# Attention inside a macaron block: the results of a pair of heads are normalised, turned and split in front of the second half of the next pair's keys

## The chip, the cores and the metric

The kernel runs on one core of a Trainium2 chip. The metric is the device time of one execution in microseconds; the lower the better. Engine names in the profile: PE is TensorE, PEld its weight load, DVE VectorE, ACT ScalarE, POOL GpSimd, SP SyncE, which here only issues DMAs.

## What is computed

x has 8 batch rows of 1024 tokens with 256 features. A feed-forward block (fp4-quantised weights and activations) is followed by attention and a second feed-forward block; each adds to x:

```python
x = x + 0.5 * ffn(layernorm(x))
x = x + attn(layernorm(x))
x = x + 0.5 * ffn(layernorm(x))
```

Attention has 16 heads of 64:

```python
q, k, v = heads(query @ Wq), heads(query @ Wk), heads(query @ Wv)
w = softmax(einsum('bhqd,bhkd->bhqk', q, k) / DH + causal)
w = w * mask                                  # a ramp over keys, one span for each head
w = w / (sum(w) + 1e-8)
out = einsum('bhqk,bhkd->bhqd', w, v)
return merge_heads(out) @ Wo
```

## The kernel before

The first feed-forward block (and the preparation of weights) takes the first 580 us, attention the stretch to about 2870 us, the second block the rest. All engines' programs are written out by hand; each engine runs its own list in order, and semaphores tie them together.

**Pairs.** Attention goes over 8 batch rows, and in each over 8 pairs of heads (`over_pairs`): 64 pairs, numbered g. A pair is a fixed list of steps that `pair_steps` makes and that TensorE, ScalarE and VectorE all read, each doing its own part of it. GpSimd and SP have lists of their own (`pair` in their blocks).

**Units and groups.** A pair has 16 units: a head a and a block j of 128 queries, in the order `ORDER`. A unit's keys (causal, so j + 1 blocks) are cut into groups of up to four blocks; `GROUPS` has 24 of them for a pair. For a unit, TensorE makes scores two units ahead (`scores`, L1398 and L1399), VectorE takes the row maximum (`row_max`, L1591), ScalarE the exponential (`exp`, L1499). For a group, TensorE transposes the exponentials (`turn`, L1409), ScalarE and VectorE split them into fp16 high and low halves (`turn_hi` L1507, `turn_lo` L1597), and TensorE multiplies with the values three groups later (`value`, L1425, LAG = 3). ScalarE copies finished results to `o_raw` (`copy_out`, L1518). The last results of a pair are thus copied behind the third group of the next.

**Side pieces.** Between these run the pieces that prepare the next pair g + 1 and finish the pair g - 1. All use one PSUM bank, `side_ps`, one after the other. A piece sits in a slot: the number of the group behind whose transposes TensorE takes it (`V_SLOTS`, `WO_SLOTS`, `FRESH_SLOTS`, filled in order by the list `pieces`). The pieces are:
- q, k: projections of the next pair's queries and keys, two halves of 512 tokens each (L1323). ScalarE copies a half to SBUF as it is (`keep_raw`, L1474), GpSimd splits it into high and low halves (`split`, L1277 and L1279), and SP places both by DMA where the scores read them (`place`, L1141): 4 DMAs for q, 8 for k, when both halves are split.
- o_turn: transposes of the normalised results of g - 1, two halves (L1364), with the same way over ScalarE and GpSimd into `oT`. The first half waits for the semaphore o_norm.
- v: the value projection for the next two pairs (L1335), in every second pair ("V pairs", odd g). wo: the output product with Wo (L1376), in the others ("W pairs", even g); its first piece waits for both halves of oT.
- x_turn: transposes of the next batch row's x, in the pair r = 6 of all batch rows but the last (`turns_rows`). These 7 are W pairs too and use `FRESH_SLOTS`, with 14 pieces.

**The result path.** When ScalarE has copied the last results of g - 1, GpSimd adds their two parts (`sums`, L1255, o_sum). VectorE makes the denominators (`normalise`: den L1604, rden L1608) behind the groups named in `NORM`. GpSimd multiplies (`outputs`, L1260, o_norm), TensorE turns the result (o_turn), ScalarE copies, GpSimd splits. GpSimd does all this in the order of its own list, in which `outputs` waits for rden and each `split` for its raw copy:

```python
for kind, c in (("q", 0), ("q", 1), ("k", 0)):
    split(kind, c, g + 1, None, None)
outputs(g - 1)
split("k", 1, g + 1, None, None)
for c in range(2):
    split("o_turn", c, None, g - 1, 1 - par)
```

Of the kernel before, what the change touches and what calls it, by code (L numbers as in the profile page):

```python
# [581 lines left out]
ORDER = (7, 0, 5, 1, 6, 3, 4, 2)  # L582
UNITS = [(a, j) for a in range(2) for j in ORDER]
GROUPS = [(n, k0, min(GROUP, j + 1 - k0)) for n, (a, j) in enumerate(UNITS) for k0 in range(0, j + 1, GROUP)]
NORM = (6, 7)
ROWS_FROM = 11

WO_SLOTS = (0, 2, 4, 7, 9, 11, 14, 15, 19, 21)
# [18 lines left out]
def starts_rows(b, r):  # L607

    return isinstance(r, int) and r == 0 and not (isinstance(b, int) and b == BATCH - 1)


def turns_rows(b, r):

    return r == PAIRS - 2 and b < BATCH - 1


def pair_steps(before, after, fresh, values, rows=False):

    q, k, v, turn_o, wo, turn_x = ([(kind, c, dg) for c in range(n)] for kind, n, dg in (
        ("q", 2, 1), ("k", 2, 1), ("v", 4, 1), ("o_turn", 2, -1), ("wo", 4, -1), ("x_turn", 4, 1)))
    pieces = (q + k if after else [None] * 4) + (turn_x if fresh else []) + (turn_o if before else [None] * 2)
    if values:
        pieces += v if after else [None] * 4
    else:
        pieces += wo if before else [None] * 4  # L630
    slots = {i: [] for i in range(NG)}
    for i, piece in zip(FRESH_SLOTS if fresh else V_SLOTS if values else WO_SLOTS, pieces, strict=True):
        slots[i].append(piece)
    steps, late_lo = [], []

    def flush(late):
        steps.extend(late)
        late.clear()

    for n in range(NU):  # L640
        more = n + 2 < NU or after
        unit = ((n + 2) % NU, (n + 2) // NU)
        if more:
            steps.append(("scores",) + unit)
        for i in [i for i, (m, _, _) in enumerate(GROUPS) if m == n]:
            first = GROUPS[i][1] == 0
            if i >= LAG or before:
                steps.append(("value", (i - LAG) % NG, (i - LAG) // NG))
                m = GROUPS[(i - LAG) % NG][0]
                if LAST_GROUP[m] == (i - LAG) % NG:  # L650
                    steps.append(("copy", m, (i - LAG) // NG))
            steps.append(("turn", i, 0))
            if i or before:
                steps.append(("lo", (i - 1) % NG, (i - 1) // NG))
            flush(late_lo)
            if first and more:
                steps.append(("max",) + unit)
            for piece in slots[i]:
                flush(late_lo)
                if piece:  # L660
                    steps.append(piece)
                    steps.append((piece[0] + "_hi",) + piece[1:])
                    late_lo.append((piece[0] + "_lo",) + piece[1:])
            if first and more:
                steps.append(("exp",) + unit)
            if before and i in NORM:
                steps.append(("norm", NORM.index(i), -1))
            if rows and i >= ROWS_FROM:
                steps.append(("norm_x", i - ROWS_FROM, 1))
    flush(late_lo)  # L670
    if not after:
        steps.append(("lo", NG - 1, 0))
        for i in range(NG - LAG, NG):
            steps.append(("value", i, 0))
            if LAST_GROUP[GROUPS[i][0]] == i:
                steps.append(("copy", GROUPS[i][0], 0))
    return steps
# [392 lines left out]
def attention(nc, block, sem, sb, src, dst, dram, keep, given):  # L1070

    tail = {}
    with ExitStack() as ctx:
# [131 lines left out]
        def _(pool):  # L1205
# [16 lines left out]
            def root(n):  # L1222
                pool.wait_ge(sem("var_eps"), n)
                nc.gpsimd.tensor_tensor(rstd[:], var_eps[:], power[:], ALU.pow).then_inc(sem("rstd"), 1)

            def masks(g, r):

                if g is not None:

                    pool.wait_ge(sem("v_masked"), g * 2)  # L1230
                    pool.sem_inc(sem("passed_pool"), 1)
                nc.gpsimd.tensor_copy(twin_mask[:], keep["mask"][:, :, bass.ds(r * 2, 4)]).then_inc(sem("twin_mask"), 2)

            def values(g, r, par):

                vc = v_cols[par]

                pool.wait_ge(sem("value_done"), g * NG - NG + AHEAD["value_done"])
                pool.sem_inc(sem("passed_pool"), 1)
                nc.gpsimd.tensor_copy(vc[:, :, :, DH], keep["mask_hi"][:, :, bass.ds(r * 2, 2)]).then_inc(sem("v_edge"), 1)  # L1240
                nc.gpsimd.tensor_copy(vc[:, :, :, VHI + DH], keep["mask_lo"][:, :, bass.ds(r * 2, 2)]).then_inc(sem("v_edge"), 1)
                for c in range(2):

                    pool.wait_ge(sem("v_masked"), 2 * g + (2 * c + 2 - 2 * par))
                    pool.sem_inc(sem("passed_pool"), 1)
                    rows = slice(c * (QT // 2), (c + 1) * (QT // 2))
                    vm = v_masked[:, rows, 2 * par:2 * par + 2, :]
                    nc.gpsimd.tensor_copy(vc[:, rows, :, 0:DH], vm).then_inc(sem("v_hi"), 1)  # L1248
                    pool.wait_ge(sem("v_hi"), 2 * g + (c + 1))
                    nc.gpsimd.tensor_tensor(vc[:, rows, :, VHI:VHI + DH], vm, vc[:, rows, :, 0:DH], ALU.subtract).then_inc(sem("v_cols"), 1)  # L1250

            def sums(g):

                pool.wait_ge(sem("o_copied"), g * NO + (NO + AHEAD["o_copied"]))
                nc.gpsimd.tensor_tensor(o_sum[:], o_raw[:, :, :VHI], o_raw[:, :, VHI:], ALU.add).then_inc(sem("o_sum"), 1)  # L1255

            def outputs(g):

                pool.wait_ge(sem("rden"), g + 1)
                nc.gpsimd.tensor_tensor(o_norm[:].rearrange("p j a d -> p a j d"), o_sum[:, :, :DH].rearrange("p (a j) d -> p a j d", a=2),  # L1260
                                        rden[:].rearrange("p (a j) -> p a j", a=2).unsqueeze(3).broadcast_to([P, 2, QT, DH]),
                                        ALU.mult).then_inc(sem("o_norm"), 1)

            def split(kind, c, g, gp, par_p):

                if kind == "o_turn":
                    hi, lo = (oT[s][:, par_p, c * GROUP:(c + 1) * GROUP].rearrange("p j n -> p (j n)") for s in range(2))
                    names, count = ("oT_hi", "oT_lo"), 2 * gp + (c + 1)

                    pool.wait_ge(sem("wo_added"), 2 * gp - (2 if par_p else 0) + AHEAD["wo_added"])  # L1270
                    pool.wait_ge(sem("o_turn_raw"), 2 * gp + (c + 1))
                else:
                    hi, lo = (side[kind][s][:, c * CHUNK:(c + 1) * CHUNK] for s in range(2))
                    names, count = (f"{kind}_hi", f"{kind}_lo"), 2 * g + (c + 1)

                    pool.wait_ge(sem(f"{kind}_raw"), 2 * g - 2 + (c + 1))
                nc.gpsimd.tensor_copy(hi, side_raw[kind][:, c]).then_inc(sem(names[0]), 1)  # L1277
                pool.wait_ge(sem(names[0]), count)
                nc.gpsimd.tensor_tensor(lo, side_raw[kind][:, c], hi, ALU.subtract).then_inc(sem(names[1]), 1)  # L1279
# [6 lines left out]
            def pair(b, r, par, before, after, fresh, twin):  # L1286
                g = b * PAIRS + r
                if after and par == 1:
                    masks(g + 1, 0 if fresh else r + 1)
                if before:  # L1290
                    sums(g - 1)
                if after:
                    for kind, c in (("q", 0), ("q", 1), ("k", 0)):
                        split(kind, c, g + 1, None, None)
                if before:
                    outputs(g - 1)
                if after:
                    split("k", 1, g + 1, None, None)
                if before:
                    for c in range(2):  # L1300
                        split("o_turn", c, None, g - 1, 1 - par)
                if after:
                    values(g + 1, 0 if fresh else r + 1, 1 - par)
                if starts_rows(b, r):
                    root(b + 2)

            pool.sem_inc(sem("o_sum"), AHEAD["o_sum"])
            pool.sem_inc(sem("oT_lo"), AHEAD["oT_lo"])
            over_pairs(pool, start, pair)
            tail["gpsimd"] = {START: lambda: sums(BATCH * PAIRS - 1), -2: lambda: outputs(BATCH * PAIRS - 1)}  # L1310

# [429 lines left out]
```

## Time and profile before

| what | value |
|---|---|
| median of 3 runs | 3377.65 us (3376.19 to 3378.86) |
| the profiled execution | 3378.71 us, of it the profile's span 3376.6 us |
| busy over the span | PE 95%, PEld 79%, DVE 81%, ACT 70%, POOL 44% |
| mean granted TensorE clock | 0.987 of full speed |
| one W pair and one V pair together | 69.9 us |

How to read it: the share of an engine is an average over three stages; attention has to be read by itself. Waits are attributed to the instruction whose semaphore came last. Ends of matmuls are modelled, so starts are the safer numbers on TensorE. "issue" as the cause of a wait means that the profile shows no releaser. Slots and groups are not named in the rows; they follow from the order of the instructions.

### The profile page before, as it was taken

What the parts mean: (1) busy time and instruction counts of PE and PEld (TensorE: products, weight loads), DVE (VectorE), ACT (ScalarE), POOL (GpSimd) and SP (SyncE); (2) the same over time, 40 slices, a digit from 0 to 9 for tenths busy, and PEclk for the clock granted to TensorE, in tenths of its full rate; (3) what the DMA queues carried; (4) which work ended last, traced back from release to release, by engine and by line L of the source; (5) the groups of instructions that cost most, each with busy time, mean ns of one, the idle gap of its engine ahead of it and who ended that gap; (6) DMA issues with size and microseconds to landing.
All of it is one profiled execution on the core that took longest, in us unless ns stands there. A gap on an engine that the chain in (4) does not pass through costs nothing.

```text
span 3376.6 us, 77211 instructions
## 1 busy us (share of the span) xinstructions
PE 3196.7 (95%) x28848; PEld 2678.6 (79%) x28848; DVE 2747.1 (81%) x5326; ACT 2365.3 (70%) x4315; POOL 1500.9 (44%) x1666
## 2 busy tenths in 40 slices
PE   4999996999999999999999999999999998799998
PEld 4999995677777777777777777777777776799998
DVE  8999984877877887787787778878777777899996
ACT  3566652777777777778777777777777777465564
POOL 2243321544545545445445455455455453233331
PEclk9999998999999999999999999999999999899999
DMA  3133212222422332332233223224222333111110
GB/s 110 49 96 95 92 63 60 63 62 57 106 56 58 79 82 58 78 78 62 62 81 79 60 63 90 60 60 105 54 57 67 82 70 107 35 57 57 57 54 32
DMA packets 160353, 235.78 MB, mean 70 GB/s; under 512 B 30064, under 2 KB 71152, under 8 KB 159728
## 3 DMA queue, kind: packets, MB, share of 16 engines
q1 hardware_dynamic: 159984, 230.84, 26.0%
q8 instruction: 234, 3.83, 0.5%
q14 instruction: 135, 1.11, 0.1%
HBM read 95.49 MB, written 34.61 MB: 39 GB/s over the span
## 4 chain that ended last, share of the span: by engine, by line
PE 68%; issue 6%; DVE 5%; ACT 2%; POOL 2%; DVEq 0%; ACTq 0%; POOLq 0%
PE at_t_ps L1409 13%; PE at_o_ps L1425 10%; PE at_side_ps L1323 10%; PE ffn_gu_ps L505 7%; PE at_s_ps L1398 6%; PE at_s_ps L1399 6%; PE at_side_ps L1376 4%; PE ffn_down_ps L530 4%; PE at_side_ps L1335 4%; DVE at_e_rows L1591 2%; PE at_side_ps L1364 2%; ACT at_eT_hi L1507 1%; PE ffn_hT_ps L475 1%; DVE at_eT_lo L1597 1%; DVE at_v_masked L1569 1%
## 5 line engine op out<-in xcount | busy, mean ns | idle before, releaser
L1597 DVE SCALAR_TENSOR_TENSOR at_eT_lo<-at_t_ps,at_eT_hi 128x512 f16<-128x512 f32 (+3 forms) x1536 | 852.7, 555 | 471.5 <-ACT at_eT_hi L1507 445.2
L1499 ACT ACTIVATE at_e_rows<-at_e_rows,at_neg_max 128x1024 f32<-128x1024 f32 (+7 forms) x1024 | 792.2, 774 | 215.9 <-DVE at_neg_max L1591 214.5
L1507 ACT ACTIVATE at_eT_hi<-at_t_ps 128x512 f16<-128x512 f32 (+3 forms) x1536 | 745.1, 485 | 190.2 <-PE at_t_ps L1409 181.3
L1591 DVE CUSTOM_DVE_ANT_0 at_e_rows<-at_s_ps,at_strip,keep_s_scale 128x1024 f32<-128x1024 f32 (+7 forms) x1024 | 827.9, 809 | 10.2 <-PE at_s_ps L1399 7.5
L1409 PE MATMUL at_t_ps<-at_ident,at_e_rows 128*128 128x128 f32 x4608 | 801.0, 284 | 0.0
L1425 PE MATMUL at_o_ps<-at_v_cols,at_eT_hi 128*128 128x132 f16 x4608 | 610.6, 221 | 11.5 <-ACT at_o_raw L1518 7.1
L1425 PE MATMUL at_o_ps<-at_v_cols,at_eT_lo 128*128 128x66 f16 x4608 | 567.9, 193 | 0.0
L1398 PE MATMUL at_s_ps<-at_kh_st,at_q_st 128*128 128x512 f16 (+3 forms) x1536 | 501.8, 327 | 18.2 <-DVE at_acc L1581 12.5
L1425 PEld LDWEIGHTS at_o_ps<-at_v_cols,at_eT_hi 128*128 128x128 f16 x4608 | 432.9, 97 | 92.0 <-DVE at_eT_lo L1597 24.5
L1409 PEld LDWEIGHTS at_t_ps<-at_ident,at_e_rows 128*128 128x128 f32 x4608 | 492.9, 141 | 3.9 <-issue 0.5
L1399 PE MATMUL at_s_ps<-at_kl_st,at_q_st 128*128 128x512 f16 (+3 forms) x1536 | 481.6, 327 | 0.0
L1425 PEld LDWEIGHTS at_o_ps<-at_v_cols,at_eT_lo 128*128 128x128 f16 x4608 | 420.6, 98 | 60.4
L385 POOL TENSOR_TENSOR ffn_h_q<-ffn_code,ffn_scale 128x704 f32<-128x704 f32 x128 | 177.8, 1391 | 572.2 <-DVE ffn_code L313 572.2
L1255 POOL TENSOR_TENSOR at_o_sum<-at_o_raw 128x1056 f32<-128x1056 f32 x64 | 132.5, 2071 | 521.5 <-ACT at_o_raw L1518 521.5
L1323 PE MATMUL at_side_ps<-at_xT_hi,at_w_qk 128*128 128x512 f16 x1012 | 343.4, 380 | 1.4 <-DVE at_xT_lo L1555 1.4
L505 PE MATMUL ffn_gu_ps<-ffn_w_gu_hi,ffn_xT_hi 128*128 128x352 f32 x1024 | 259.3, 335 | 28.8 <-DVE ffn_raw L276 18.0
L505 PE MATMUL ffn_gu_ps<-ffn_w_gu_lo,ffn_xT_hi 128*128 128x352 f32 x1024 | 252.1, 328 | 0.0
L505 PE MATMUL ffn_gu_ps<-ffn_w_gu_hi,ffn_xT_lo 128*128 128x352 f32 x1024 | 251.9, 328 | 0.0
L1248 POOL CAST at_v_cols<-at_v_masked 128x512 f16<-128x512 f32 x128 | 78.3, 612 | 375.8 <-DVE at_v_masked L1569 375.8
L442 ACT ACTIVATE ffn_silu<-ffn_gu_ps 128x704 f32<-128x704 f32 x128 | 97.1, 758 | 211.2 <-PE ffn_gu_ps L505 211.2
L1398 PEld LDWEIGHTS at_s_ps<-at_kh_st,at_q_st 128*128 128x128 f16 x1536 | 154.6, 101 | 104.8 <-DVE at_acc L1581 13.9
L1399 PEld LDWEIGHTS at_s_ps<-at_kl_st,at_q_st 128*128 128x128 f16 x1536 | 150.5, 98 | 92.1 <-issue 1.1
(226 smaller groups left out, 6957.7 us busy)
## 6 DMA issues: line engine op xcount, KB each, us to landing
at_kh_st<-at_k_hi SPq DMA_DIRECT2D x256, 128.0 KB, 2.3
at_kl_st<-at_k_lo SPq DMA_DIRECT2D x256, 128.0 KB, 2.4
at_w_qk<-w_qk_split SPq DMA_DIRECT2D x65, 256.0 KB, 3.0
at_q_st<-at_q_hi SPq DMA_DIRECT2D x128, 128.0 KB, 2.4
at_q_st<-at_q_lo SPq DMA_DIRECT2D x128, 128.0 KB, 2.4
at_w_v<-w_v_split SPq DMA_DIRECT2D x66, 128.0 KB, 2.4
ffn_x_rows<-in_L_attn_query_dram SPq DMA_DIRECT2D x32, 256.0 KB, 3.2
ffn_x_res<-in_L_attn_query_dram SPq DMA_DIRECT2D x32, 256.0 KB, 3.8
```

Source lines behind the costliest of these rows:

```text
L385: nc.gpsimd.tensor_tensor(blocks_of(h_q[:, par, j, :INNER]), blocks_of(code[:, j * INNER:(j + 1) * INNER]), per_block(scale[:, par, j * HB ...
L505: last = nc.tensor.matmul(gu_ps[:, c, 0:HALF_I], xT[a][:, par, kt, j * P:(j + 1) * P], gu[b][:, kt, c * HALF_I:(c + 1) * HALF_I], start=n ...
L530: last = nc.tensor.matmul(down_ps[:, j * HID:(j + 1) * HID], hT[a][:, j, kt, :], down[b][:, kt, :], start=n == 0, stop=n == len(passes) - 1)
L1323: last = nc.tensor.matmul(bank[:], wts[:, w, s, kt, :], xT[t][:, kt, c * CHUNK:(c + 1) * CHUNK], start=i == 0, stop=i == len(passes) - 1)
L1398: nc.tensor.matmul(out, qs, kh_st[par][a][:, k0:k0 + w], start=True, stop=False)
L1399: last = nc.tensor.matmul(out, qs, kl_st[par][a][:, k0:k0 + w], start=False, stop=True)
L1409: last = nc.tensor.transpose(t_ps[i % TBUF][:, b * P:(b + 1) * P], e_rows[:, n % 4, (k0 + b) * P:(k0 + b + 1) * P], ident[:])
L1425: last = nc.tensor.matmul(o[:, :VPART[s]], eT[s][:, i % EBUF, b * P:(b + 1) * P], v_cols[par][:, k0 + b, a, :VPART[s]], start=k0 + b == 0 ...
L1499: nc.scalar.activation(e_rows[:, n % 4, :w], e_rows[:, n % 4, :w], ACT.Exp, bias=neg_max[:, n % 4:n % 4 + 1], scale=-1.0).then_inc(sem("ex ...
L1507: nc.scalar.activation(eT[0][:, i % EBUF, :count * P], t_ps[i % TBUF][:, :count * P], ACT.Copy, scale=PSCALE).then_inc(sem("eT_hi"), 1)
L1591: nc.vector.tensor_tensor_reduce(e_rows[:, n % 4, :w], s_ps[n % 2][:, col:col + w], strip[:, SEQ - w:], keep["s_scale"][:, 0:1], BIGGEST, ...
L1597: nc.vector.scalar_tensor_tensor(out=eT[1][:, i % EBUF, :count * P], in0=t_ps[i % TBUF][:, :count * P], scalar=PSCALE, in1=eT[0][:, i % EB ...
```

## The change

In `pair_steps`, the turn of the results (o_turn, two halves) moves in front of the second half of k: the pieces of a pair are now q, q, k, o_turn, o_turn, k in slots 2, 3, 5, 7, 9, 11 (V pairs) or 0, 2, 4, 7, 9, 11 (W pairs), where k had slot 7 and o_turn slots 9 and 11. In the 7 pairs that turn x the pieces keep their order. `NORM` puts den behind group 5 and rden behind group 6, one group earlier each, in all pairs. GpSimd's list gets `outputs` in front of both halves of k, and the splits of o_turn in front of the second half of k (in the pairs that turn x: outputs, both halves of k, then o_turn).

```diff
--- before.py
+++ after.py
@@ -582,7 +582,7 @@
 ORDER = (7, 0, 5, 1, 6, 3, 4, 2)
 UNITS = [(a, j) for a in range(2) for j in ORDER]
 GROUPS = [(n, k0, min(GROUP, j + 1 - k0)) for n, (a, j) in enumerate(UNITS) for k0 in range(0, j + 1, GROUP)]
-NORM = (6, 7)
+NORM = (5, 6)
 ROWS_FROM = 11
 
 WO_SLOTS = (0, 2, 4, 7, 9, 11, 14, 15, 19, 21)
@@ -623,7 +623,8 @@
 
     q, k, v, turn_o, wo, turn_x = ([(kind, c, dg) for c in range(n)] for kind, n, dg in (
         ("q", 2, 1), ("k", 2, 1), ("v", 4, 1), ("o_turn", 2, -1), ("wo", 4, -1), ("x_turn", 4, 1)))
-    pieces = (q + k if after else [None] * 4) + (turn_x if fresh else []) + (turn_o if before else [None] * 2)
+    q, k, turn_o = (kind if have else [None] * 2 for kind, have in ((q, after), (k, after), (turn_o, before)))
+    pieces = q + k + turn_x + turn_o if fresh else q + k[:1] + turn_o + k[1:]
     if values:
         pieces += v if after else [None] * 4
     else:
@@ -1290,15 +1291,19 @@
                 if before:
                     sums(g - 1)
                 if after:
-                    for kind, c in (("q", 0), ("q", 1), ("k", 0)):
-                        split(kind, c, g + 1, None, None)
+                    for c in range(2):
+                        split("q", c, g + 1, None, None)
                 if before:
                     outputs(g - 1)
+                turned_late = turns_rows(b, r)
                 if after:
-                    split("k", 1, g + 1, None, None)
+                    for c in range(2 if turned_late else 1):
+                        split("k", c, g + 1, None, None)
                 if before:
                     for c in range(2):
                         split("o_turn", c, None, g - 1, 1 - par)
+                if after and not turned_late:
+                    split("k", 1, g + 1, None, None)
                 if after:
                     values(g + 1, 0 if fresh else r + 1, 1 - par)
                 if starts_rows(b, r):
```

How it moves instructions, at three places of the same W pair (g = 12). GpSimd, from the sum of results onward, before and after (lines behind 600 have moved by 1, those behind 1290 by 5):

```order
L1255 TENSOR_TENSOR at_o_sum<-at_o_raw 128x1056
L1277 CAST at_q_hi<-at_raw_q 128x512
L1279 TENSOR_TENSOR at_q_lo<-at_raw_q,at_q_hi 128x512
L1277 CAST at_q_hi<-at_raw_q 128x512
L1279 TENSOR_TENSOR at_q_lo<-at_raw_q,at_q_hi 128x512
L1277 CAST at_k_hi<-at_raw_k 128x512
L1279 TENSOR_TENSOR at_k_lo<-at_raw_k,at_k_hi 128x512
L1260 TENSOR_TENSOR at_o_norm<-at_o_sum,at_rden 128x2x8x64
L1277 CAST at_k_hi<-at_raw_k 128x512
L1279 TENSOR_TENSOR at_k_lo<-at_raw_k,at_k_hi 128x512
L1277 CAST at_oT_hi<-at_raw_o_turn 128x512
L1279 TENSOR_TENSOR at_oT_lo<-at_raw_o_turn,at_oT_hi 128x512
```

```order
L1256 TENSOR_TENSOR at_o_sum<-at_o_raw 128x1056
L1278 CAST at_q_hi<-at_raw_q 128x512
L1280 TENSOR_TENSOR at_q_lo<-at_raw_q,at_q_hi 128x512
L1278 CAST at_q_hi<-at_raw_q 128x512
L1280 TENSOR_TENSOR at_q_lo<-at_raw_q,at_q_hi 128x512
L1261 TENSOR_TENSOR at_o_norm<-at_o_sum,at_rden 128x2x8x64
L1278 CAST at_k_hi<-at_raw_k 128x512
L1280 TENSOR_TENSOR at_k_lo<-at_raw_k,at_k_hi 128x512
L1278 CAST at_oT_hi<-at_raw_o_turn 128x512
L1280 TENSOR_TENSOR at_oT_lo<-at_raw_o_turn,at_oT_hi 128x512
L1278 CAST at_oT_hi<-at_raw_o_turn 128x512
L1280 TENSOR_TENSOR at_oT_lo<-at_raw_o_turn,at_oT_hi 128x512
```

The normalisation (o_norm) has moved up by one split, and the split of the second half of k down behind both halves of oT.

VectorE, around den and rden, before and after (`ISA at_e_rows` is a row maximum; that of 128x640, of unit 6, is taken in group 6, that of 128x512 in group 5):

```order
L1591 ISA at_e_rows,at_neg_max<-at_s_ps,at_strip,keep_s_scale 128x512
L1591 ISA at_neg_max 128x1
L1597 SCALAR_TENSOR_TENSOR at_eT_lo<-at_t_ps,at_eT_hi 128x256
L1591 ISA at_e_rows,at_neg_max<-at_s_ps,at_strip,keep_s_scale 128x640
L1591 ISA at_neg_max 128x1
L1604 SCALAR_TENSOR_TENSOR at_den<-at_o_sum 128x16
L1597 SCALAR_TENSOR_TENSOR at_eT_lo<-at_t_ps,at_eT_hi 128x512
L1608 RECIPROCAL at_rden<-at_den 128x16
```

```order
L1596 ISA at_e_rows,at_neg_max<-at_s_ps,at_strip,keep_s_scale 128x512
L1596 ISA at_neg_max 128x1
L1609 SCALAR_TENSOR_TENSOR at_den<-at_o_sum 128x16
L1602 SCALAR_TENSOR_TENSOR at_eT_lo<-at_t_ps,at_eT_hi 128x256
L1596 ISA at_e_rows,at_neg_max<-at_s_ps,at_strip,keep_s_scale 128x640
L1596 ISA at_neg_max 128x1
L1613 RECIPROCAL at_rden<-at_den 128x16
L1602 SCALAR_TENSOR_TENSOR at_eT_lo<-at_t_ps,at_eT_hi 128x512
```

den stands behind the maximum that is one earlier, and rden directly behind the maximum of 128x640, where den stood.

TensorE, in slot 7, before and after:

```order
L1409 MATMUL at_t_ps<-at_ident,at_e_rows 128x128 x3
L1323 MATMUL at_side_ps<-at_xT_hi,at_w_qk_52 128x512
L1323 MATMUL at_side_ps<-at_xT_lo,at_w_qk_52 128x512
L1323 MATMUL at_side_ps<-at_xT_hi,at_w_qk_52 128x512 x2
L1323 MATMUL at_side_ps<-at_xT_lo,at_w_qk_52 128x512
L1323 MATMUL at_side_ps<-at_xT_hi,at_w_qk_52 128x512
L1398 MATMUL at_s_ps<-at_kh_st_7431,at_q_st_7427 128x384
L1399 MATMUL at_s_ps<-at_kl_st_7435,at_q_st_7427 128x384
```

```order
L1414 MATMUL at_t_ps<-at_ident,at_e_rows 128x128 x3
L1369 MATMUL at_side_ps<-at_ident,at_o_norm 128x128 x4
L1403 MATMUL at_s_ps<-at_kh_st_7431,at_q_st_7427 128x384
L1404 MATMUL at_s_ps<-at_kl_st_7435,at_q_st_7427 128x384
```

The six matmuls of k's second half have made room for four transposes of o_norm; the scores of 128x384 behind them are the same.

## Rows read from the trace of the kernel before

**Rows 1.** the page, section 1: busy us (share of the span) xinstructions

```profile
PE 3196.7 (95%) x28848; PEld 2678.6 (79%) x28848; DVE 2747.1 (81%) x5326; ACT 2365.3 (70%) x4315; POOL 1500.9 (44%) x1666
```

**Rows 2.** windows of attention: us, busy us of each engine, granted clock, DMA

```profile
700.00:2800.00 2100.00, 2050.41 (x20349) 1595.92 (x20348) 1658.32 (x3828) 1627.13 (x3203) 1082.09 (x1211) 1.00 0.29 70
```

**Rows 3.** waits of TensorE, 620 to 2860 us: total, times, longest

```profile
PE at_side_ps L1376 <- issue: 22.6, 31, 1.0
...
PE at_s_ps L1398 <- DVE at_acc L1581: 12.5, 6, 2.1
```

**Rows 4.** timeline of TensorE, W pair: start us, us, instruction [idle before]

```profile
1022.74 0.38 PE L1323 MATMUL at_side_ps<-at_xT_hi,at_w_qk 128*128 128x512 f16 x1
...
1028.36 0.60 PE L1364 MATMUL at_side_ps<-at_ident,at_o_norm 128*128 128x128 f32 x4
...
1031.47 0.30 PE L1409 MATMUL at_t_ps<-at_ident,at_e_rows 128*128 128x128 f32 x1
...
1032.43 0.38 PE L1376 MATMUL at_side_ps<-at_w_out,at_oT_hi 128*128 128x256 f16 x2 [0.65 <-issue]
```

**Rows 5.** timeline of GpSimd, the same pair

```profile
1021.14 1.16 POOL L1279 TENSOR_TENSOR at_q_lo<-at_raw_q,at_q_hi 128x512 f16<-128x512 f32 x1
...
1024.05 1.91 POOL L1260 TENSOR_TENSOR at_o_norm<-at_o_sum,at_rden 128x1024 f32<-128x1024 f32 x1
...
1031.16 1.16 POOL L1279 TENSOR_TENSOR at_oT_lo<-at_raw_o_turn,at_oT_hi 128x512 f16<-128x512 f32 x1
```

**Rows 6.** timeline of VectorE, the W pair and the V pair behind it

```profile
1022.66 0.23 DVE L1604 SCALAR_TENSOR_TENSOR at_den<-at_o_sum 128x16 f32<-128x16 f32 x1
...
1057.44 0.18 DVE L1604 SCALAR_TENSOR_TENSOR at_den<-at_o_sum 128x16 f32<-128x16 f32 x1
...
1058.67 0.24 DVE L1608 RECIPROCAL at_rden<-at_den 128x16 f32<-128x16 f32 x1
```

**Rows 7.** timelines of TensorE and GpSimd, the V pair

```profile
1057.77 0.38 PE L1323 MATMUL at_side_ps<-at_xT_hi,at_w_qk 128*128 128x512 f16 x1
...
1058.99 1.90 POOL L1260 TENSOR_TENSOR at_o_norm<-at_o_sum,at_rden 128x1024 f32<-128x1024 f32 x1 [0.34 <-DVE at_rden L1608]
```

**Rows 8.** SP's DMAs and TensorE's scores, W pair; page: us to landing

```profile
1027.79 2.38 SPq L1141 DMA_DIRECT2D at_kh_st<-at_k_hi  x4
...
1030.21 2.54 SPq L1141 DMA_DIRECT2D at_kl_st<-at_k_lo  x4
...
1042.16 0.38 PE L1398 MATMUL at_s_ps<-at_kh_st,at_q_st 128*128 128x512 f16 x1
...
at_kl_st<-at_k_lo SPq DMA_DIRECT2D x256, 128.0 KB, 2.4
```

**Rows 9.** windows right behind the six waits of 2.1 us, columns as Rows 2

```profile
906.00:910.00 4.00, 3.63 (x36) 2.77 (x37) 4.00 (x12) 1.91 (x5) 0.00 (x0) 1.00 0.63 182
...
1192.00:1196.00 4.00, 3.73 (x23) 3.04 (x24) 3.47 (x12) 1.45 (x4) 0.00 (x0) 0.57 0.66 204
...
1479.00:1483.00 4.00, 3.56 (x36) 2.70 (x37) 4.00 (x12) 1.90 (x5) 0.00 (x0) 1.00 0.60 177
...
1766.00:1769.00 3.00, 3.00 (x22) 2.80 (x20) 2.91 (x9) 1.58 (x3) 0.00 (x0) 0.50 0.85 269
...
2053.00:2056.00 3.00, 3.00 (x20) 2.61 (x19) 2.53 (x9) 0.97 (x3) 0.00 (x0) 0.51 0.72 240
...
2340.00:2343.00 3.00, 3.00 (x35) 2.39 (x34) 3.00 (x10) 1.18 (x3) 0.00 (x0) 1.00 0.80 215
```

**Rows 10.** timeline of GpSimd: sums around a wait with drop, and without

```profile
1160.25 2.07 POOL L1255 TENSOR_TENSOR at_o_sum<-at_o_raw 128x1056 f32<-128x1056 f32 x1 [3.47 <-ACT at_o_raw L1518]
...
1234.04 2.07 POOL L1255 TENSOR_TENSOR at_o_sum<-at_o_raw 128x1056 f32<-128x1056 f32 x1 [3.47 <-ACT at_o_raw L1518]
...
1447.43 2.08 POOL L1255 TENSOR_TENSOR at_o_sum<-at_o_raw 128x1056 f32<-128x1056 f32 x1 [3.47 <-ACT at_o_raw L1518]
...
1519.85 2.07 POOL L1255 TENSOR_TENSOR at_o_sum<-at_o_raw 128x1056 f32<-128x1056 f32 x1 [3.47 <-ACT at_o_raw L1518]
```

## The prediction

> **What bounds the kernel now.** I read the page first. TensorE is busy 95% of the span [rows 1], which alone says little, since ends of matmuls are modelled. So I looked at attention by itself: from 700 to 2800 us TensorE is busy 2050.4 of 2100 us and idle 49.6, while VectorE, ScalarE and GpSimd are busy 79, 77 and 52% of it [rows 2]. Then the waits of TensorE inside attention: the largest is 22.6 us in 31 waits before the output product (L1376), the second 12.5 us in 6 waits of up to 2.1 us, once per batch row, before scores [rows 3]. Attention is thus a stream of matmuls in a fixed order with 0.8 us of idleness per pair of heads: whatever holds TensorE there lengthens the kernel, and there is little idleness later that could pay it back.
>
> The reader should next look at one pair with output pieces (a "W pair", from 1013 us) and the pair behind it (a "V pair", value pieces). In the W pair TensorE ends the transpose of group 14 at 1031.47 + 0.30 = 1031.77 and then starts its output product only at 1032.43 [rows 4]; over all 31 W pairs that is 22.6 / 31 = 0.73 us each [rows 3]. GpSimd shows why: its last low half of oT ends at 1031.16 + 1.16 = 1032.32 [rows 5]. The result path (sum, normalise, turn, split) ends 0.11 us before the product starts. This wait the change can take away. The price stands in the same two views: slot 7 of the order, where the turn of the results goes, is reached by TensorE at 1022.74 (k, second half, today), while the normalised results are ready only at 1024.05 + 1.91 = 1025.96 [rows 4, 5].
>
> **The change part by part.** Counts first. 63 pairs have results of a pair before them: 32 V pairs, 31 W pairs; 7 of the W pairs also turn the next batch row's x, and there only the denominators and GpSimd's order move. So the new piece order is in 32 V and 24 W pairs. No instruction is added or dropped.
>
> 1. *Denominators one group up (VectorE).* den takes the place behind the row maximum of group 5, rden the place behind that of group 6, where den is today. That place is at 1022.66 in the W pair and at 1057.44 in the V pair [rows 6]. den in front of it pushes it back by about its own 0.18 us. rden takes 0.24 us, GpSimd starts 0.08 us behind its end (1058.67 + 0.24 = 1058.91 against 1058.99) [rows 6, 7]. So normalisation can start at 1022.66 + 0.18 + 0.24 + 0.08 = 1023.16 in W and at 1057.94 in V. The two VectorE instructions are the same as today; VectorE is not the bound, so nothing for them.
>
> 2. *Normalisation in front of the first half of the keys (GpSimd).* GpSimd's last half of q ends at 1021.14 + 1.16 = 1022.30 [rows 5], so GpSimd waits 0.86 us for rden. It now has no split of k in between. Normalisation takes 1.91 us and TensorE follows 0.11 us later (1032.32 against 1032.43): the results are usable at 1025.18 in W and 1057.94 + 1.90 + 0.11 = 1059.95 in V. The first half of the keys is split some 1.9 us later; only the placing DMAs want it, and these wait for the second half anyway.
>
> 3. *Turn of the results in slots 7 and 9 (TensorE).* TensorE arrives in slot 7 at 1022.74 (W) and 1057.77 (V) [rows 4, 7]. Everything behind it on its queue (scores of unit 7, value of group 5, transposes of group 8) waits too. New wait: 1025.18 - 1022.74 = **2.44 us** in each W pair, 1059.95 - 1057.77 = **2.18 us** in each V pair. In sum 24 x 2.44 + 32 x 2.18 = 58.6 + 69.8 = **+128.4 us**. In the 7 x-turning pairs the results are turned in slots 12 and 14, far behind: 0.
>
> 4. *The wait before the output product.* The split of the second result half ends some two slots earlier while TensorE comes 2.4 us later, so it is gone: 24 x 0.73 = **-17.5 us**. In the 7 x-turning pairs it stays.
>
> 5. *Second half of the keys in slot 11.* Work of TensorE moves, 0. Behind it: ScalarE's copy, GpSimd's split, eight placing DMAs on SP, then scores of the next pair. In the W pair TensorE reaches slot 11 at 1028.36 today, and then at 1028.36 - 0.83 (1.30 of k for 0.47 of a turn in slot 7) + 2.44 = 1029.97 [rows 4]. k takes 1.3 us; from the end of a side piece in that slot to the end of its split there are now about 3.4 us (1028.96 to 1032.32), so k is split at about 1034.7. The eight DMAs take 4.96 us to issue (1027.79 to 1032.75) and the last lands 2.4 us after its issue began (0.6 us before the end of the eight), so near 1041.5 [rows 8]. Scores of the next pair start at 1042.16 today [rows 8], then at 1042.16 + 2.44 - 0.73 = 1043.9. Margin 2.4 us, so I take 0. The two steps are estimates worked out from these rows; 1 us more still fits. If that cover is gone, the next bill comes there (a rival).
>
> 6. *TensorE's clock.* The trace has a test of what a wait of this size does: the six waits of 2.1 us at the batch rows [rows 3]. Right behind three of them the granted clock is 0.50 to 0.57, the half level (1.2 GHz), behind the other three 1.00 (2.4 GHz) [rows 9]. From the sum two pairs ahead of such a wait to the sum behind it are 1234.04 - 1160.25 = 73.79 us with the drop and 1519.85 - 1447.43 = 72.42 us without [rows 10], so a drop costs **1.37 us**. The new waits are of the same length: 56 x 3/6 x 1.37 = **+38.4 us**. Bounds: none (0), and all 56 at a full loss of half of 3.4 us, 95. I take the middle because the rows are of waits as long as the new ones.
>
> A rule speaks otherwise here: the Trainium skill, page "TensorE: Matmul & The Clock Gate", section "Why this matters for your kernels", advises keeping idle gaps between bursts of matmuls short, and the gaps that it counts as harmful are longer than any of the new waits. By it term 6 would be 0. The rows do not agree with it: half of the waits of 2.1 us were followed by the lower clock.
>
> Sum against the profiled execution: 3378.7 + 128.4 - 17.5 + 38.4 = 3528.0 us. It lies 1.1 above the median of the runs shown, so against that: **3527 us**, 4.4% slower.
>
> **The rivals.**
> - *The clock holds.* Terms 1 to 5 alone: 3378.7 + 110.9 = 3489.6, or 3489 against the median. For it: three of six waits left the clock alone, and the sample is small. Against: the other three. The section of the Trainium skill named above speaks for this one.
> - *Idle time pays some back.* 49.6 us of idleness lie in attention [rows 2]; without the waits before output products 27.0 remain. Even with all of it paid back the result is near 3500. It bounds the gain rather than making a case.
> - *Every stall is followed by a drop, or the keys land late too.* The W pair's margin of term 5 is the thinnest spot; a further 1 us in 56 pairs is 56 us, and drops behind all stalls add 38 more than taken. 3580 or so. Against: the margin of 2.4 us, and 3 of 6.
> - *Faster.* The wait on the normalised results never appears, and only the wait of 0.73 us goes: 3378.7 - 17.5 = 3361, or 3360 against the median. This needs o_norm to be finished when TensorE reaches slot 7, so to start by 1020.7 in the W pair. It decides at rden: with its place in VectorE's order behind the maximum of group 6, where den starts at 1022.66 today, it can't be done before 1022.9, and GpSimd is itself in the halves of q until 1022.30 [rows 5, 6]. Only a TensorE that comes 2 us later to slot 7, for a reason that I overlooked, would save it.
>
> **How the numbers follow.** About 0.2% (7 us) is what a measurement of this kernel can tell from no change. Forecast (stalls of 2.2 to 2.4 us, about half with a clock drop, 3505 to 3555): 0.60. Clock holds, or idleness pays back (3470 to 3505): 0.17. More drops or late keys (3555 to 3600): 0.13. Partly hidden stall (half of it, about 3430): 0.04. Same: 0.02. Faster: 0.04. The range from 3460 to 3585 leaves out the last three cases and the upper edge of the one before, about 0.17. All cases but the last two are slower: 0.94; they are 0.60 + 0.17 + 0.13 + 0.04.
>
> **What the profile of the changed kernel would show.** TensorE before the turn of o_norm: a wait released by GpSimd, some 56 times, 2.2 to 2.4 us each, near 128 us in all. GpSimd before o_norm: 0.8 us for rden in most W pairs. The waits before the output product: 7 instead of 31. The distance of two sums over a V and a W pair grows from 69.9 us by some 3.8 without drops. In attention the clock row shows more nines and eights, and half-clock stretches right behind stalls. TensorE's wait before scores of a next pair on anything of k's DMAs would show term 5 wrong. The prediction is wrong if TensorE does not wait for o_norm, if it waits under 1 us, or if fewer than 10 or more than 45 drops follow.

## The result and the profile after

| what | before | after |
|---|---|---|
| median | 3377.53 us (4 runs, 3376.19 to 3378.86) | 3532.07 us (4 runs, 3518.49 to 3545.78) |
| ratio | 1 | 1.0458, 95% interval 1.0402 to 1.0513 |
| profiled execution, its span | 3378.71, 3376.6 us | 3518.49, 3516.4 us |
| mean granted TensorE clock | 0.987 | 0.976 |

The changed kernel is 4.6% slower; 3527 us had been forecast. The executions after lie at two places, two near 3519 and two near 3545; the profiled one is of the lower place.

The page of the changed kernel, section 1, beside [rows 1]: TensorE has the same instructions and a smaller share of a longer span.

```profile
PE 3222.1 (92%) x28848; PEld 2700.8 (77%) x28848; DVE 2771.4 (79%) x5326; ACT 2375.2 (68%) x4315; POOL 1503.2 (43%) x1666
```

The waits of TensorE from 600 to 3010 us, beside [rows 3] (engine, line, releaser: total, times, longest):

```profile
PE at_side_ps L1369 <- POOL at_o_norm L1261: 133.0, 56, 2.9
PE at_s_ps L1403 <- DVE at_acc L1586: 12.5, 6, 2.1
PE at_side_ps L1381 <- issue: 7.1, 7, 1.0
```

The first row is new: 133.0 us in 56 waits, as many as pairs with the new order. The wait before scores, 12.5 us in 6, is unchanged. The 31 waits before the output product have become 7, those of the pairs that turn x.

TensorE in slot 7 of the same W pair as in [rows 4] (its sum starts at 1038.60 now), then in the V pair behind it:

```profile
1044.34 0.52 PE L1414 MATMUL at_t_ps<-at_ident,at_e_rows 128*128 128x128 f32 x3
1047.74 1.09 PE L1369 MATMUL at_side_ps<-at_ident,at_o_norm 128*128 128x128 f32 x4 [2.88 <-POOL at_o_norm L1261]
...
1085.65 0.63 PE L1369 MATMUL at_side_ps<-at_ident,at_o_norm 128*128 128x128 f32 x4 [1.98 <-POOL at_o_norm L1261]
```

TensorE is idle for 2.88 us where k's second half used to start at once, and for 1.98 us in the V pair. The four transposes behind the wait take 1.09 us in the W pair and 0.63 in the V pair: the clock has dropped in the first. GpSimd, the same W pair, beside [rows 5]:

```profile
1043.11 1.17 POOL L1280 TENSOR_TENSOR at_q_lo<-at_raw_q,at_q_hi 128x512 f16<-128x512 f32 x1
1045.69 1.90 POOL L1261 TENSOR_TENSOR at_o_norm<-at_o_sum,at_rden 128x1024 f32<-128x1024 f32 x1 [1.42 <-DVE at_rden L1613]
```

GpSimd ends q at 1044.28 and stands 1.42 us before it can normalise. The reason is on VectorE, beside [rows 6] (first piece the W pair, second piece the V pair):

```profile
1043.33 0.98 DVE L1609 SCALAR_TENSOR_TENSOR at_den<-at_o_sum 128x16 f32<-128x16 f32 x1
...
1045.37 0.24 DVE L1613 RECIPROCAL at_rden<-at_den 128x16 f32<-128x16 f32 x1
...
1082.04 0.18 DVE L1609 SCALAR_TENSOR_TENSOR at_den<-at_o_sum 128x16 f32<-128x16 f32 x1
...
1083.28 0.25 DVE L1613 RECIPROCAL at_rden<-at_den 128x16 f32<-128x16 f32 x1
```

den takes 0.98 us in the W pair and 0.18 in the V pair; before the change it takes 0.18 to 0.46 in all pairs. It starts at 1043.33, 0.22 us behind the start of GpSimd's subtraction for q's second half (1043.11 to 1044.28), and ends 0.03 us after its end. The lengths of pairs, as sums on GpSimd, beside [rows 10]:

```profile
964.84 2.08 POOL L1256 TENSOR_TENSOR at_o_sum<-at_o_raw 128x1056 f32<-128x1056 f32 x1 [3.47 <-ACT at_o_raw L1523]
...
1000.78 2.08 POOL L1256 TENSOR_TENSOR at_o_sum<-at_o_raw 128x1056 f32<-128x1056 f32 x1 [13.91 <-ACT at_o_raw L1523]
...
1038.60 2.08 POOL L1256 TENSOR_TENSOR at_o_sum<-at_o_raw 128x1056 f32<-128x1056 f32 x1 [3.47 <-ACT at_o_raw L1523]
...
1076.15 2.08 POOL L1256 TENSOR_TENSOR at_o_sum<-at_o_raw 128x1056 f32<-128x1056 f32 x1 [13.92 <-ACT at_o_raw L1523]
```

A V pair takes 1038.60 - 1000.78 = 37.82 us (before 36.09 or 36.10: 1.72 more), a W pair 1000.78 - 964.84 = 35.94 (33.77 before: 2.17 more), and the next W pair 1076.15 - 1038.60 = 37.55. The last has a clock drop behind its wait, 1.61 us more than the one without. Not every drop costs that much: in the last batch row, where the clock falls 0.65 us before the wait ends instead of 0.1, the four W pairs with a drop take 37.27 to 37.29 us, 1.33 more. The granted clock, in windows behind the V wait that ends at 1010.28 and the W wait that ends at 1047.74, columns as in [rows 2]:

```profile
1010.30:1013.30 3.00, 3.00 (x30) 2.38 (x31) 1.38 (x4) 1.98 (x4) 2.84 (x4) 1.00 0.00 0
1048.00:1051.00 3.00, 3.00 (x16) 2.26 (x15) 0.63 (x2) 1.25 (x3) 2.57 (x4) 0.50 0.02 6
```

Counted over all waits in the clock record of this trace, 18 of 25 waits of 2.7 to 2.9 us are followed by the half clock (1.2 GHz), none of 31 waits of 1.98 us, and all six of 2.08 us at the batch rows (three before).

### The profile page after: what moved, and what is told of

The parts are those of the page before. It is cut to its first block, busy times and chain, and to the rows that moved or that the text cites. A ratio compares the mean times of both kernels' runs of the same rounds, so it can differ in the third digit from the quotient of the medians.

```text
span 3516.4 us, 77211 instructions
## 1 busy us (share of the span) xinstructions
PE 3222.1 (92%) x28848; PEld 2700.8 (77%) x28848; DVE 2771.4 (79%) x5326; ACT 2375.2 (68%) x4315; POOL 1503.2 (43%) x1666
## 4 chain that ended last, share of the span: by engine, by line
PE 64%; DVE 7%; issue 6%; POOL 4%; ACT 3%; ACTq 0%; DVEq 0%; POOLq 0%
PE at_t_ps L1414 12%; PE at_o_ps L1430 9%; PE at_side_ps L1328 8%; PE ffn_gu_ps L505 7%; PE at_s_ps L1403 6%; PE at_s_ps L1404 6%; PE at_side_ps L1381 4%; PE ffn_down_ps L530 4%; PE at_side_ps L1340 4%; POOL at_o_norm L1261 3%; DVE at_e_rows L1596 3%; PE at_side_ps L1369 2%; ACT at_eT_hi L1512 2%; DVE at_eT_lo L1602 2%; PE ffn_hT_ps L475 1%
## 5 line engine op out<-in xcount | busy, mean ns | idle before, releaser
L1414 PE MATMUL at_t_ps<-at_ident,at_e_rows 128*128 128x128 f32 x4608 | 810.6, 287 | 0.0
L1403 PE MATMUL at_s_ps<-at_kh_st,at_q_st 128*128 128x512 f16 (+3 forms) x1536 | 509.5, 332 | 18.2 <-DVE at_acc L1586 12.5
L1414 PEld LDWEIGHTS at_t_ps<-at_ident,at_e_rows 128*128 128x128 f32 x4608 | 501.2, 143 | 0.6 <-issue 0.5
```

Source lines behind the costliest of these rows:

```text
L1403: nc.tensor.matmul(out, qs, kh_st[par][a][:, k0:k0 + w], start=True, stop=False)
L1414: last = nc.tensor.transpose(t_ps[i % TBUF][:, b * P:(b + 1) * P], e_rows[:, n % 4, (k0 + b) * P:(k0 + b + 1) * P], ident[:])
```

## The experiments

All were timed against the kernel before, whose median was 3378.0 to 3378.4 us in all of these comparisons. "Changed kernel" is the one with the whole change. Where waits for o_norm are summed, the single wait of 10.5 or 10.6 us for the last results, at the end of attention, which every version has, is taken off. Theory: the time is that of TensorE's waits for o_norm, less the waits before the output product, plus clock drops. Rivals: the late second half of the keys, or the denominators' load on VectorE.

**1. The order alone.** The changed kernel with `NORM` as it was.

```diff
-NORM = (5, 6)
+NORM = (6, 7)
```

> The new order of pieces and of GpSimd's list, with den and rden left behind groups 6 and 7. Theory (TensorE's wait for o_norm in slot 7 is the cost): rden ends 7.24 us behind the start of the sum in the W pair and 8.50 in the V pair, as before; normalisation takes 1.9, so TensorE waits about 3.1 us in 24 W and 3.2 us in 32 V pairs, 177 us in all against 133 in the changed kernel; with more clock drops 3570 to 3620 us. Rival (the late second half of the keys is the cost): the keys stand where they stand in the changed kernel, so the time stays near 3532.

Measured: 3584.4 us, ratio 1.0620 (1.0603 to 1.0636). TensorE's waits for o_norm, up to 3200 us:

```profile
PE at_side_ps L1369 <- POOL at_o_norm L1261: 184.8, 57, 10.6
```

That is 174.2 us in 56 waits (177 expected), 3.1 us each in both kinds of pair. The second half of the keys stands where it stands in the changed kernel and the time is 52 us more, so the time does not go by the place of the keys; that this place costs nothing is shown by experiment 8, which keeps it. Moving the denominators up, which is part of the change, saved these 52 us of the harm.

**2. The denominators alone.** The kernel before with `NORM = (5, 6)`.

> The old order of pieces and of GpSimd's list, den and rden one group up. Theory: TensorE never waits for o_norm in slot 9 and does not now either; 3378 us within 5. In the W pair den meets GpSimd's split of q and takes about 1.0 us as in the changed kernel, but VectorE has room for it. Rival (the denominators disturb VectorE, which is near its limit): 24 times 0.8 us show, 3397.

Measured: 3378.3 us, ratio 1.0003 (0.9994 to 1.0012). den in the W pair, and GpSimd at that moment:

```profile
1016.76 0.96 DVE L1604 SCALAR_TENSOR_TENSOR at_den<-at_o_sum 128x16 f32<-128x16 f32 x1
...
1016.51 1.16 POOL L1279 TENSOR_TENSOR at_q_lo<-at_raw_q,at_q_hi 128x512 f16<-128x512 f32 x1
```

den is long again (0.96 us, to 1017.72; GpSimd's subtraction to 1017.67), and costs nothing where TensorE does not wait for what follows it. So the rival of VectorE's load falls.

**3. Why den is long.** The changed kernel with both steps behind group 6.

```diff
-            if before and i in NORM:
-                steps.append(("norm", NORM.index(i), -1))
+            if before and i == 6:
+                steps.extend([("norm", 0, -1), ("norm", 1, -1)])
```

> The changed kernel with den and rden both behind group 6, so den later by one group, rden in its place. If den is long in the W pairs (0.98 us) because it meets GpSimd's subtraction for the second half of q, it is short again here (0.2 us), rden ends about 6.5 us behind the start of the sum instead of 7.0, and the W pair's wait shrinks from 2.87 to about 2.4 us although den comes later; the V pair's wait grows from 1.98 to about 2.2. Sum of waits near 127 instead of 133. Time 3510 to 3545. If den is long for another reason (its data, its place), the W wait grows to 3.4 us or more and the time goes up by 15 or more.

Measured: 3520.5 us, ratio 1.0427 (1.0411 to 1.0443). VectorE and TensorE in the W pair at 1041.51:

```profile
1047.53 0.18 DVE L1609 SCALAR_TENSOR_TENSOR at_den<-at_o_sum 128x16 f32<-128x16 f32 x1
1047.75 0.25 DVE L1613 RECIPROCAL at_rden<-at_den 128x16 f32<-128x16 f32 x1
...
1050.13 1.09 PE L1369 MATMUL at_side_ps<-at_ident,at_o_norm 128*128 128x128 f32 x4 [2.35 <-POOL at_o_norm L1261]
```

den comes a group later, when GpSimd has ended q, and is short; rden ends 6.49 us behind the start of the sum instead of 7.02, and the wait is 2.35 instead of 2.88 us. All waits for o_norm come to 124.4 us in 56 (127 expected). So den is held by what GpSimd is doing, not by its data. Both of its inputs are columns of o_sum in SBUF. The Trainium skill, page "SBUF — State Buffer", section "Who interferes with whom", says that a VectorE instruction with two SBUF inputs contends with a GpSimd instruction that reads SBUF, and calls the ports that the two engines share an exclusive lock. The rows agree in three kernels (the changed one, experiments 2 and 8): den ends 0.03 to 0.05 us behind the GpSimd instruction that had started before it.

**4. The clock.** The changed kernel with transposes that nobody reads, in TensorE's time of waiting.

```diff
+                    for i in range(fill[0] if c == 0 else 0):
+                        nc.tensor.transpose(bank[:, i % GROUP * P:(i % GROUP + 1) * P], ident[:], ident[:])
                     if c == 0:
                         pe.wait_ge(sem("o_norm"), gp + 1)
...
+                fill[0] = 0 if turns_rows(b, r) else 14 if par else 20
```

> The changed kernel with 20 (W) or 14 (V) transposes of the identity that nobody reads in front of the wait for o_norm, 2.3 or 1.6 us of TensorE's time that it would spend waiting. They end before o_norm does, so the path is the same. Theory (the clock drops behind the waits are a cost of their own): the drops go, the time falls to 3490 to 3500 us and its executions lie together, instead of at 3518 and 3545. If the drops cost nothing in the end, or the waits alone make the spread: 3518 to 3545 as in the changed kernel. The extra transposes are not part of the computation.

Measured: 3487.8 us, ratio 1.0326 (1.0310 to 1.0342), all four executions within 3485.5 to 3489.0. Windows from 700 to 2800 us, this kernel and then the changed one, columns as in [rows 2]:

```profile
700.00:2800.00 2100.00, 2045.78 (x20199) 1613.58 (x20198) 1601.78 (x3653) 1557.81 (x3054) 1035.25 (x1156) 1.00 0.28 68
```

```profile
700.00:2800.00 2100.00, 1952.64 (x19136) 1521.08 (x19134) 1581.84 (x3607) 1540.79 (x3018) 1025.43 (x1143) 0.98 0.28 67
```

With the same path the time is 31 us less than the lower place of the changed kernel and 57 less than the upper one, and the spread is gone. The granted clock of the stretch is 1.00 again instead of 0.98: no half clock follows a turn of o_norm any more, except for the last one of attention, and the six behind the waits at the batch rows remain. So without the drops behind o_norm the change costs some 110 us, and these drops cost 30 to 60. Up to 5 us of this are not the clock: o_norm's turn starts 0.10 us sooner behind the sum when TensorE is at work (9.04 against 9.14 us in the W pair, 56 times).

**5. A smaller wait.** The first turn in slot 8 instead of 7 (`WO_SLOTS` and `V_SLOTS`).

> The changed kernel with the first turn of the results in slot 8 instead of 7. TensorE has group 8 to do before it (about 1.0 us). Theory: each wait for o_norm shrinks by 1.0 us, to 1.9 (W) and 1.0 (V), 77 us in all; the clock falls less often; 3440 to 3465 us. Rival (late keys, order of pieces): as the changed kernel, 3532.

Measured: 3439.7 us, ratio 1.0181 (1.0166 to 1.0197); waits up to 3010 us:

```profile
PE at_side_ps L1369 <- POOL at_o_norm L1261: 90.7, 57, 10.6
```

80.1 us of waiting in 56 are left of 133.0, and the time follows: 79 us less than the lower place of the changed kernel for 53 us less of waiting. The rest fits the drops: 24 waits in the changed kernel (18 for o_norm, six at the batch rows) and 5 here (four and one) are followed by the half clock, and 19 drops at 1.33 to 1.61 us are 25 to 31 us.

**6. No wait on o_norm, turns in slots 9 and 10.** Here the expectation failed.

> The changed kernel with the turns in slots 9 and 10, the second half of the keys still behind both in slot 11. Theory: o_norm is ready 9.0 to 9.4 us behind the start of the sum, TensorE arrives at 8.8 (W) and 10.0 (V), so it waits 0.4 us at most, and the wait before the output product is gone; 3378 - 17 + 8 = 3369, at most 3378. Rival (the late second half of the keys is a cost of its own): slower than before, as it stays late.

Measured: 3435.8 us, ratio 1.0171 (1.0157 to 1.0184). Waits of TensorE up to 3010 us:

```profile
PE at_side_ps L1328 <- ACT at_raw_o_turn L1479: 29.6, 55, 0.5
PE at_side_ps L1369 <- ACT at_raw_o_turn L1479: 29.3, 56, 0.6
PE at_o_ps L1430 <- ACT at_o_raw L1523: 17.5, 35, 1.0
```

o_norm is no longer waited for, and 111 waits on ScalarE's raw copies stand in its place, 59 us. Side pieces share one bank; a piece in the slot right behind another comes 0.5 us before the bank is copied out. This happens twice in each pair (turn behind turn, k behind turn). These 59 us and 10 more on the third row than before (17.5 against 7.1), less 15.5 won before the output product, are some 54 of the 57 us by which this kernel is slower than the one before. Against experiment 8, which is 84 us faster, the rows explain 69, and the rest is open. No row names a DMA of the keys, so the rival that predicted a slower kernel was right on the time and not on the cause.

**7. The wait before the output product, moved from.** The kernel before, wo one slot later.

```diff
-WO_SLOTS = (0, 2, 4, 7, 9, 11, 14, 15, 19, 21)
+WO_SLOTS = (0, 2, 4, 7, 9, 11, 15, 16, 19, 21)
-FRESH_SLOTS = (0, 2, 3, 5, 6, 8, 9, 11, 12, 14, 16, 18, 20, 21)
+FRESH_SLOTS = (0, 2, 3, 5, 6, 8, 9, 11, 12, 14, 17, 18, 20, 21)
```

> The kernel before with the first output product in slot 15 instead of 14 (17 instead of 16 in the pairs that turn x), nothing else. Theory: its wait for the split results (22.6 us in 31) is all that the change could win; one group later it is covered: 3378 - 22 = 3356, at least 3363 if half stays. If the wait is paid back elsewhere: 3378.

Measured: 3388.5 us, ratio 1.0030 (1.0019 to 1.0040): 10 us slower, where a gain of 15 to 22 had been expected. Waits:

```profile
PE at_o_ps L1425 <- ACT at_o_raw L1518: 24.8, 33, 1.0
PE at_side_ps L1376 <- DVE at_acc L1581: 13.4, 24, 1.1
...
PE at_side_ps L1376 <- issue: 1.8, 7, 0.3
```

The wait goes (1.8 us left), and 13.4 us before the second product and 17.7 more us before value matmuls (24.8 against 7.1) pay back more than was won. I had not priced the neighbour in slot 16 and the copy of results.

**8. The change with o_norm in time.** The changed kernel, the denominators behind groups 3 and 4, and on GpSimd the normalisation in front of q's second half.

```diff
-NORM = (5, 6)
+NORM = (3, 4)
...
-                    for c in range(2):
-                        split("q", c, g + 1, None, None)
+                    split("q", 0, g + 1, None, None)
                 if before:
                     outputs(g - 1)
+                if after:
+                    split("q", 1, g + 1, None, None)
```

> The changed kernel with the denominators behind groups 3 and 4 and the normalisation in front of the second half of the queries on GpSimd. den can only start at the sum's end (2.1 us) and may be held by GpSimd's split of q until 3.9; rden then ends near 4.5, o_norm near 6.5, so TensorE waits 0.4 us in slot 7 of the W pair and not in the V pair. 3365 to 3380. If VectorE is held up and passes it on: over 3390.

Measured: 3351.8 us, ratio 0.9916 (0.9903 to 0.9930): 0.8% faster than the kernel before, and 13 us under the range that I had expected. GpSimd (with the sums of the pairs beside it), TensorE and VectorE in the W pair at 1011.05:

```profile
975.41 2.08 POOL L1256 TENSOR_TENSOR at_o_sum<-at_o_raw 128x1056 f32<-128x1056 f32 x1 [13.81 <-ACT at_o_raw L1524]
...
1011.05 2.08 POOL L1256 TENSOR_TENSOR at_o_sum<-at_o_raw 128x1056 f32<-128x1056 f32 x1 [3.47 <-ACT at_o_raw L1524]
1013.07 0.61 POOL L1278 CAST at_q_hi<-at_raw_q 128x512 f16<-128x512 f32 x1
1013.76 1.16 POOL L1280 TENSOR_TENSOR at_q_lo<-at_raw_q,at_q_hi 128x512 f16<-128x512 f32 x1
1014.88 1.91 POOL L1261 TENSOR_TENSOR at_o_norm<-at_o_sum,at_rden 128x1024 f32<-128x1024 f32 x1
...
1043.94 2.08 POOL L1256 TENSOR_TENSOR at_o_sum<-at_o_raw 128x1056 f32<-128x1056 f32 x1 [13.81 <-ACT at_o_raw L1524]
...
1017.15 0.60 PE L1370 MATMUL at_side_ps<-at_ident,at_o_norm 128*128 128x128 f32 x4
...
1013.16 0.56 DVE L1610 SCALAR_TENSOR_TENSOR at_den<-at_o_sum 128x16 f32<-128x16 f32 x1
```

o_norm ends at 1016.79 and TensorE turns it at 1017.15 without a wait. den, in the last row, is held to 1013.72, the end of GpSimd's cast (1013.07 + 0.61), not to the end of the subtraction, so rden is sooner than I had expected. The pairs are not only free of the wait for o_norm but shorter than before: the W pair takes 1043.94 - 1011.05 = 32.89 us (33.77 before: 0.88 less), the V pair 1011.05 - 975.41 = 35.64 (0.45 less).

**9. Which part of 8 wins.** The same with the pieces in the old order.

```diff
-    pieces = q + k + turn_x + turn_o if fresh else q + k[:1] + turn_o + k[1:]
+    pieces = q + k + (turn_x if fresh else []) + turn_o
```

> The fast version (denominators behind groups 3 and 4, normalisation before the second half of q) with the pieces of TensorE, ScalarE and VectorE in the old order (second half of k in slot 7, turns in 9 and 11); GpSimd's list is as in the fast version, so its split of k's second half stands behind the splits of the results. Theory: the new piece order is what wins, once nothing waits for o_norm; with the old order the wait before the output product is back, 22 us, and the time is 3370 to 3385. Rival (the early normalisation itself wins, by what it takes off GpSimd and VectorE): 3345 to 3360.

Measured: 3378.3 us, ratio 1.0002 (0.9993 to 1.0011); the wait is back:

```profile
PE at_side_ps L1382 <- issue: 22.6, 31, 1.0
```

The pairs have their old lengths (33.77 us for a W pair, 36.09 for a V pair). The order of pieces wins 26.5 us, on condition that o_norm is ready in slot 7; early normalisation by itself wins nothing. By the lengths of pairs the order wins 24 x 0.88 + 32 x 0.45 = 35.5 us; of the difference, five more drops (six waits at the batch rows are followed by the half clock in experiment 8, one here) are some 7 us. Only 0.65 us of the 0.88 in the W pair is the wait before the output product, and of the 0.45 in the V pair 0.14 is a shorter wait before the value product (L1341, 0.15 against 0.29 us); the cause of the rest is open.

**10. and 11. Either half of 8's remedy.** The changed kernel with `NORM = (3, 4)` only, and kernel 8 with `NORM = (5, 6)`.

> The changed kernel with den and rden behind groups 3 and 4; GpSimd still splits both halves of q first. rden is ready when GpSimd ends q (5.7 us behind the start of the sum), so o_norm ends near 7.6 and TensorE waits 1.6 us in slot 7 of the W pair and 0.3 in the V pair: 48 us in all. Theory: 3378 + 48 - 20 = 3406, with few clock drops, 3395 to 3415. If the place of rden and not GpSimd's queue were the bound: 3355; if the order of pieces were the cost: 3500 or more.

> The fast version with the denominators where the changed kernel has them, behind groups 5 and 6. GpSimd stands idle in front of normalisation until rden ends 6.3 (W, if den is short because GpSimd does not run) or 7.4 us (V) behind the sum's start; TensorE waits 2.2 to 2.4 us (W) and 2.0 (V), 120 us. Theory: 3378 + 120 - 16 + clock = 3495 to 3545: GpSimd's place alone wins nothing. Rival (GpSimd's queue alone is the bound): near 3352.

Measured: 3394.8 us, ratio 1.0048 (1.0033 to 1.0064), and 3517.4 us, ratio 1.0414 (1.0398 to 1.0430). Waits of the one, up to 3010 us, and of the other, up to 3200 us:

```profile
PE at_side_ps L1369 <- POOL at_o_norm L1261: 49.5, 47, 10.6
```

```profile
PE at_side_ps L1370 <- POOL at_o_norm L1261: 125.7, 57, 10.5
```

With rden early, GpSimd's queue is the bound: 49.5 - 10.6 = 38.9 us of waiting are left, where 48 had been expected. With rden late, 115.2 us in 56 are left (120 expected), and GpSimd's free place is worth 15 us of the 180 between the changed kernel and experiment 8. Both are needed.

**12. The changed kernel again.**

> The changed kernel itself once more: its executions lay at 3518 and 3545. Theory (the waits are the same in every execution and only the number of clock drops differs): the waits of TensorE for o_norm add up to the same 132 us in 56, at either level, and an execution at 3545 shows a granted clock of 0.967 against 0.976.

Measured: 3540.5 us (3537.9 to 3550.3), ratio 1.0493; the profiled execution took 3538.35 at a mean clock of 0.970. Waits up to 3010 us:

```profile
PE at_side_ps L1369 <- POOL at_o_norm L1261: 134.0, 56, 2.9
...
PE at_side_ps L1381 <- issue: 7.1, 7, 1.0
```

It is 134.0 us in 56 against 133.0: all waits have the same length but four of 2.2 us, which were 1.98. The 20 us more of time come with more half clock (0.970 against 0.976): 28 of the 56 waits for o_norm are followed by it here, 18 in the first execution. So the places of the executions differ by drops.

## Why the prediction was right

The mechanism was right: TensorE waits for o_norm in slot 7, once in each of the 56 pairs, and experiments 1, 5, 8, 10 and 11 change only how late o_norm is against that slot and move the time with it. That 3527 lies 5 us from 3532 is in part luck, since several terms were off in opposite directions.

- *Denominators up (step 1).* Right in V: rden ended 7.37 us behind the sum's start, where 7.45 was forecast. Mis-sized in W: den was taken at 0.18 us and measured 0.98, since its new place is beside GpSimd's split of q; rden ended at 7.02 where 6.44 had been worked out. I had counted its price on VectorE (nothing, experiment 2 agrees) and not that a place beside GpSimd changes its length.
- *Normalisation and turn (steps 2, 3).* 128.4 us forecast, 133.0 in the rows: 24 x 2.87 and 32 x 1.98 (one of these 2.7). The rows count from the modelled end of the last matmul. By starts, TensorE comes 3.04 us later in the W pair (9.14 - 6.10 behind the sum) against 2.44, and 2.14 in the V pair against 2.18, which makes 24 x 3.04 + 32 x 2.14 = 141.4 us.
- *The wait before the output product (step 4).* It went where forecast, 31 to 7. These waits were 22.6 - 7.1 = 15.5 us, not 17.5, since the seven that stay are the longest. But the new order gives back twice what was forecast: 0.88 us in a W pair and 0.45 in a V pair, 35.5 us, by the lengths of pairs in experiment 8. The V pair had been taken at nothing.
- *Keys in slot 11 (step 5).* k's split ended 18.0 us behind the sum in a W pair without a drop, 18.1 was worked out, and no DMA of the keys is waited for.
- *Sum of 1 to 5.* 110.9 forecast; 24 x 2.17 + 32 x 1.72 = 107.1 us by the lengths of pairs, and 110 by experiment 4. This is luck: the delay was 13 us larger than forecast and what the order gives back 18 us larger (141.4 - 35.5 = 105.9). The kinds of pair show it too: W pairs grew by 2.17 where 2.44 - 0.73 = 1.71 was forecast, V pairs by 1.72 where it was 2.18.
- *The clock (step 6).* 38.4 forecast; the profiled execution has 139.8 - 107.1 = 32.7, that of run 12 has 3538.4 - 3378.7 - 107.1 = 52.6. The price was about right, 1.33 to 1.61 us for a drop against 1.37. The share of one half was a guess from six waits: 18 of 56 in the profiled execution (18 of 25 behind the longer waits, none of 31 behind the shorter), to which three more at the batch rows come, and 28 of 56 in run 12. The forecast lies between the two executions. The advice of the Trainium skill, page "TensorE: Matmul & The Clock Gate", section "Why this matters for your kernels", by which no drop was due, does not fit these counts.
- *The faster rival* needed o_norm ready when TensorE reaches slot 7. Experiment 8 makes it so, with a different kernel, and its 3351.8 us are 9 below what the rival had named, by the return in step 4 that was sized too small.

## What to carry to other kernels

A producer's step that is moved ahead in a fixed order helps only if its input is ready by then: read the time at which the consumer's engine reaches the new slot and the time at which the input is ready, from the same timeline, and multiply the difference by the count. Here this gave 128.4 us of waits where the rows show 133.0, and it also named the remedy, both the denominators and GpSimd's queue. When a piece is moved, look at its neighbours as well: on the shared bank (experiments 6 and 7 missed there), and on the engine beside which a short instruction comes to stand (den).

## What was not expected

- den, 16 values in each partition, takes 0.98 instead of 0.18 us when GpSimd's subtraction started 0.22 us before it. The short instruction pays for the rest of the long one.
- The length of a wait does not tell whether the clock falls behind it. Waits of 1.98 us brought it down in 0 of 31 in the profiled execution and in 16 of 31 in experiment 11; waits of 2.87 us did in 17 of 24; and the six waits of 2.08 us before scores, the same in both kernels, had 3 drops before, 6 in the changed kernel and 2 in run 12. The count varies between executions of one kernel and moves the time by 20 to 30 us, which no row on waits shows.
- A version with the change's order and an early o_norm beats the kernel before by 26.6 us.
